# Attention products with 264 columns for 258, padded rows of the values and the probabilities, and 24 unread products at the end

## The reference, cut to what matters

```
h = layernorm(x) * (1 + ca) + sa
scores = einsum('nsd,ntd->nst', h * w_lhs, h * w_rhs)
attn = softmax(scores, axis=2)
x = x + ga * einsum('nst,ntd->nsd', attn, h)
h = layernorm(x) * (1 + cb) + sb
x = x + gb * (relu(h @ W1 + b1) @ W2 + b2)
```

## The kernel before, in words

| operand | starts at, modulo 256 |
|---|---|
| W1hi, W1lo, W2hi, W2lo (rows of G, weights of F) | 128 |
| hid_hi, hid_lo, h2hi, h2lo | 192 |
| Lhi, Llo, Rhi, Rlo | 64 |
| Phi[t], Plo[t], before | 64 |
| V[t] front half, V[t] rear half, before | 64 + 32 t, 80 + 32 t |
| Phi[t], Plo[t], changed | 128 + 64 t, 64 + 64 t |
| V[t] front half, V[t] rear half, changed | 64 + 64 t, 128 + 64 t |

## Time and profile before

### The profile page before, as it was taken

How to read it: one execution, slowest core, us unless ns; L and a number is a source line. 1 busy time by engine, 2 the same in 40 slices (tenths; PEclk the granted TensorE clock), 3 DMA queues, 4 the chain that set the end, 5 groups by cost and what they waited for, 6 DMA issues and landing times.

```text
span 672.1 us, 13438 instructions
## 1 busy us (share of the span) xinstructions
PE 665.8 (99%) x4481; PEld 612.9 (91%) x4481; DVE 549.5 (82%) x1139; ACT 513.4 (76%) x763; POOL 299.3 (45%) x311
## 2 busy tenths in 40 slices
PE   8999999999999999999999999999999999999998
PEld 8688898998999999999999989999899999999997
DVE  4799879998899789997899898998899977787321
ACT  2367779994899769995899948998599976677463
POOL 3471365155543364523547245352554333625444
PEclk9999999999999999999999999999999999999999
DMA  8141665237732578135662267513773246401300
GB/s 293 55 87 63 196 181 181 80 126 241 184 109 95 137 237 234 47 118 157 189 207 78 94 220 212 130 62 128 254 203 70 96 158 178 140 17 65 101 33 32
DMA packets 76929, 92.27 MB, mean 137 GB/s; under 512 B 9120, under 2 KB 67040, under 8 KB 76896
## 3 DMA queue, kind: packets, MB, share of 16 engines
q1 hardware_dynamic: 76896, 91.85, 45.4%
HBM read 55.33 MB, written 36.50 MB: 137 GB/s over the span
## 4 chain that ended last, share of the span: by engine, by line
PE 97%; DVE 2%; DMA 1%; issue 0%; SPq 0%; ACT 0%; DVEq 0%; ACTq 0%
PE col L675 9%; PE col L674 9%; PE col L673 9%; PE acc L595 8%; PE score L775 8%; PE acc L596 8%; PE acc L601 8%; PE score L771 8%; PE score L772 8%; PE score L663 4%; PE score L662 4%; PE score L664 4%; PE score L764 4%; PE score L636 2%; DMA S<-wmod 1%; PE score L751 1%
## 5 line engine op out<-in xcount | busy, mean ns | idle before, releaser
L1264 POOL TENSOR_TENSOR hid_lo<-hid,hid_hi 128x512 fp32r<-128x512 f32 x127 | 177.6, 1407 | 202.1 <-ACT hid_hi L800 201.7
L796 ACT ACTIVATE hid<-col,b1T 128x512 f32<-128x512 f32 x128 | 87.0, 679 | 69.9 <-PE col L675 65.2
L595 PE MATMUL acc<-W2hi,hid_hi 128*128 128x256 f32 x480 | 117.1, 278 | 0.0
L596 PE MATMUL acc<-W2lo,hid_hi 128*128 128x256 f32 x480 | 116.7, 278 | 0.0
L771 PE MATMUL score<-V,Phi 128*128 128x258 f32 x448 | 108.7, 281 | 0.0
L772 PE MATMUL score<-V,Phi 128*128 128x256 f32 x448 | 108.5, 281 | 0.0
L675 PE MATMUL col<-h2hi,W1lo 128*128 128x512 f32 x256 | 100.9, 394 | 0.0
L674 PE MATMUL col<-h2lo,W1hi 128*128 128x512 f32 x256 | 100.6, 393 | 0.0
L673 PE MATMUL col<-h2hi,W1hi 128*128 128x512 f32 x256 | 100.4, 392 | 0.0
L800 ACT ACTIVATE hid_hi<-hid 128x512 fp32r<-128x512 f32 x128 | 81.0, 633 | 15.3 <-PE acc L601 11.1
L595 PEld LDWEIGHTS acc<-W2hi,hid_hi 128*128 128x128 f32 x480 | 90.3, 188 | 2.5
(11 more groups left out here) (168 smaller groups left out, 1470.5 us busy)
## 6 DMA issues: line engine op xcount, KB each, us to landing
block_rows<-blocks SPq DMA_DIRECT2D x29, 512.0 KB, 2.6
blocks<-block_rows SPq DMA_DIRECT2D x116, 128.0 KB, 2.9
x_cur<-x SPq DMA_DIRECT2D x16, 512.0 KB, 4.1
ln_t<-x SPq DMA_DIRECT2D x14, 512.0 KB, 4.6
score_blocks<-stage SPq DMA_DIRECT2D x14, 512.0 KB, 3.0
S<-score_blocks SPq DMA_DIRECT2D x56, 128.0 KB, 3.6
S<-quarter_blocks SPq DMA_DIRECT2D x56, 96.0 KB, 2.3
out<-x_mlp SPq DMA_DIRECT2D x8, 512.0 KB, 3.6
```

The lines of the kernel that those rows point to most:

```text
L595: nc.tensor.matmul(o, hi, W2hi[:, it, :], start=(it == 0 and (apart or t % 2 == 0)), stop=False, skip_group_check=True)
L596: nc.tensor.matmul(o, hi, W2lo[:, it, :], start=False, stop=False, skip_group_check=True)
L796: nc.scalar.activation(hid[:, n % 2, :], col[n % 2][:], ACT.Relu, bias=b1T[:, n % FT:n % FT + 1]).then_inc(col_read, 1)
L1264: G.tensor_tensor(hid_lo[:, n % RING, :], hid[:, n % 2, :], hid_hi[:, n % RING, :].bitcast(F32), ALU.subtract).then_inc(hid_lo_done, 1)
```

## The change

- L771 and L775 stream 264 columns instead of 258, into PSUM tiles of 264 columns. Columns 258 to 263 of V are set to zero once, and their products are not read. The 8 of L772 keep 256 columns.
- Rows of V are 528 numbers (2112 bytes) instead of 520. The hi half, with the ones, now stands in front and the lo half 272 numbers (1088 bytes) behind it; L771 streams hi and L772 lo.
- Phi, Plo and `soft` are rows of 400 numbers (1600 bytes) for each t, which hold the three slots side by side. A tile of eight t is then eight pieces of 128, a row apart, for every instruction of ScalarE and VectorE on it.
- Small buffers move into the gaps and two are added, so that big buffers keep their distance to each other modulo 512 bytes, except the three rearranged ones (table above).
- `stage` and `stage_lr` now overlap every slot of Phi, so both waits stand before slot 0.
- Behind GT come 24 matmuls into `col[0]` that nobody reads: 8 of 258 columns, 8 of 260 and 8 of 256, of W2hi and W2lo with hid_hi and hid_lo as weights.

```diff
-    VW = D + 2
-    VP = D + 4
+    VW, VZ = D + 2, D + 8
+    VL, VROW = D + 16, 2 * D + 16
+    RROW = RING * P + 16
...
+        by_slot = lambda rows: rows[:, :, 0:RING * P].rearrange("p t (s c) -> p s t c", c=P)
...
-                nc.sbuf_tensor("stage_lr", [P, T, P], F32) as stage_lr, nc.sbuf_tensor("soft", [P, RING, T, P], F32) as soft:
-            stage_q = [q.rearrange("p a b -> p (a b)")[:, 0:Q * TURNS * QP] for q in (soft[:, RING - 1], stage_lr[:])]
-        Phi, Plo = sb("Phi", [P, RING, T, P], F32R), sb("Plo", [P, RING, T, P], F32R)
+        with nc.sbuf_tensor("stage", [P, 2, Q, HT, 2, QP], F32) as stage, nc.sbuf_tensor("stage_lr", [P, T, P], F32) as stage_lr, \
+                nc.sbuf_tensor("behind_stage", [P, 240], F32), nc.sbuf_tensor("soft_rows", [P, T, RROW], F32) as soft_rows:
+            soft = by_slot(soft_rows[:])
+            stage_q = [q[:].rearrange("p a b -> p (a b)")[:, 0:Q * TURNS * QP] for q in (soft_rows, stage_lr)]
+        Phi = by_slot(sb("Phi_rows", [P, T, RROW], F32R)[:])
+        mv2, nm2, rs2, nb2 = sb("mv2", [P, T, 2]), sb("nm2", [P, T]), sb("rs2", [P, T]), sb("nb2", [P, T])
+        sb("behind_Phi", [P, 72])
+        Plo = by_slot(sb("Plo_rows", [P, T, RROW], F32R)[:])
...
-        V = sb("V", [P, T, 2 * VP], F32R)
+        V = sb("V", [P, T, VROW], F32R)
...
-        av_ps = [score[0][:, 0:VW], score[0][:, HR:HR + VW]]
+        av_ps = [score[0][:, 0:VZ], score[0][:, HR:HR + VZ]]
...
+                        mv, unread = W2hi[:].rearrange("p i d -> p (i d)"), col[0]
+                        for width in (258,):
+                            for t in range(1, 5):
+                                cols = slice(t % HT * P, (t % HT + 1) * P)
+                                nc.tensor.matmul(unread[:, 0:width], hid_hi[:, 0, cols], mv[:, t * D - 2:t * D - 2 + width], start=True, stop=True)
+                                nc.tensor.matmul(unread[:, 0:D], hid_hi[:, 0, cols], W2lo[:, t, :], start=True, stop=True)
+                            for t in range(1, 5):
+                                cols = slice(t % HT * P, (t % HT + 1) * P)
+                                nc.tensor.matmul(unread[:, 0:width], hid_lo[:, 0, cols], mv[:, t * D - 2:t * D - 2 + width], start=True, stop=True)
...
                         for t in range(T):
-                            nc.tensor.matmul(o, Phi[:, slot, t, :], V[:, t, 0:VW], start=(t == 0), stop=False)
-                            nc.tensor.matmul(o[:, 0:D], Phi[:, slot, t, :], V[:, t, VP:VP + D], start=False, stop=False)
+                            nc.tensor.matmul(o, Phi[:, slot, t, :], V[:, t, 0:VZ], start=(t == 0), stop=False)
+                            nc.tensor.matmul(o[:, 0:D], Phi[:, slot, t, :], V[:, t, VL:VL + D], start=False, stop=False)
                         pe.wait_ge(plo_done, T * (b - 1) + n + 1)
                         for t in range(T):
-                            last = nc.tensor.matmul(o, Plo[:, slot, t, :], V[:, t, VP:VP + VW], start=False, stop=(t == T - 1))
+                            last = nc.tensor.matmul(o, Plo[:, slot, t, :], V[:, t, 0:VZ], start=False, stop=(t == T - 1))
...
-                        nc.scalar.activation(V[:, n * HT:(n + 1) * HT, VP:VP + D], ln_v[:], ACT.Copy).then_inc(v_hi, 1)
+                        nc.scalar.activation(V[:, n * HT:(n + 1) * HT, 0:D], ln_v[:], ACT.Copy).then_inc(v_hi, 1)
...
-                        if n == 1:
+                        if n == 0:
 
                             act.wait_ge(stage_stored[1], 16 * b)
-                        elif n == 2:
-
                             act.wait_ge(quarter_stored[1], 16 * b)
...
-                        for half in range(2):
-                            V_.memset(V[:, :, half * VP + D:half * VP + D + 1].bitcast(F32), 1.0)
-                            V_.memset(V[:, :, half * VP + D + 1:half * VP + VW].bitcast(F32), 0.0)
+                        V_.memset(V[:, :, D:D + 1].bitcast(F32), 1.0)
+                        V_.memset(V[:, :, D + 1:VZ].bitcast(F32), 0.0)
```

More of the change, by code:

```diff
@@ L279, in block_kernel @@
         lower = s_flat[:, at + 2 * TURNS * P:T * ROWS].rearrange("p (h u v t r) -> p h u v t r", h=2, u=Q, v=HT, t=2)
+        half_power, root_power = sb("half_power", [P, HT]), sb("root_power", [P, 2, DK])
         with nc.sbuf_tensor("W1_sb", [P, DK, FF], F32) as W1_sb, nc.sbuf_tensor("W2_sb", [P, FT, D], F32) as W2_sb:
             pass
[L286 to L289 removed]
+        by_slot = lambda rows: rows[:, :, 0:RING * P].rearrange("p t (s c) -> p s t c", c=P)
[7 more added lines that the diff above has]
+        Plo = by_slot(sb("Plo_rows", [P, T, RROW], F32R)[:])
         with nc.sbuf_tensor("L_first", [P, DK, ROWS], F32) as L_first, nc.sbuf_tensor("R_first", [P, DK, ROWS], F32) as R_first:
@@ L293, in block_kernel @@
         Rhi, Rlo = sb("Rhi", [P, DK, ROWS], F32R), sb("Rlo", [P, DK, ROWS], F32R)
-        with nc.sbuf_tensor("V_unsplit", [P, T, 2 * VP], F32) as V_unsplit:
-            V_first = V_unsplit[:, :, VP:VP + VW]
-        V = sb("V", [P, T, 2 * VP], F32R)
-        sb("behind_V", [P, 96])
+        with nc.sbuf_tensor("V_unsplit", [P, T, VROW], F32) as V_unsplit:
+            V_first = V_unsplit[:, :, 0:VW]
+        V = sb("V", [P, T, VROW], F32R)
+        nm1, rs1, nb1, row_max = sb("nm1", [P, T]), sb("rs1", [P, T]), sb("nb1", [P, T]), sb("row_max", [P, T])
         x_cur = sb("x_cur", [P, T, D])
@@ L692, in part @@
                             last.then_inc(tile_done, 1)
+                        mv, unread = W2hi[:].rearrange("p i d -> p (i d)"), col[0]
[7 more added lines that the diff above has]
+                                nc.tensor.matmul(unread[:, 0:width], hid_lo[:, 0, cols], mv[:, t * D - 2:t * D - 2 + width], start=True, stop=True)
+                        mv, unread = W2hi[:].rearrange("p i d -> p (i d)"), col[0]
+                        for width in (260,):
+                            for t in range(1, 5):
+                                cols = slice(t % HT * P, (t % HT + 1) * P)
+                                nc.tensor.matmul(unread[:, 0:width], hid_hi[:, 0, cols], mv[:, t * D - 0:t * D - 0 + width], start=True, stop=True)
+                                nc.tensor.matmul(unread[:, 0:D], hid_hi[:, 0, cols], W2lo[:, t, :], start=True, stop=True)
+                            for t in range(1, 5):
+                                cols = slice(t % HT * P, (t % HT + 1) * P)
+                                nc.tensor.matmul(unread[:, 0:width], hid_lo[:, 0, cols], mv[:, t * D - 0:t * D - 0 + width], start=True, stop=True)
                     elif kind == "MA":
@@ L750, in part @@
                         for t in range(HT):
-                            nc.tensor.matmul(av_ps[n], S[:, t, n * P:(n + 1) * P], V_first[:, t, :], start=(t == 0), stop=False)
+                            nc.tensor.matmul(av_ps[n][:, 0:VW], S[:, t, n * P:(n + 1) * P], V_first[:, t, :], start=(t == 0), stop=False)
                     elif kind == "AV":
@@ L763, in part @@
                                     pe.wait_ge(exp_done, n + 1)
-                                last = nc.tensor.matmul(o, S[:, t, n * P:(n + 1) * P], V_first[:, t, :], start=(t == 0), stop=(t == T - 1))
+                                last = nc.tensor.matmul(o[:, 0:VW], S[:, t, n * P:(n + 1) * P], V_first[:, t, :], start=(t == 0), stop=(t == T - 1))
                             last.then_inc(av_done, 1)
@@ L1147, in part @@
                         dve.wait_ge(v_hi, 2 * b + n - 1)
-                        V_.tensor_tensor(V[:, tiles, 0:D], ln_v[:], V[:, tiles, VP:VP + D].bitcast(F32), ALU.subtract).then_inc(v_done, 1)
+                        V_.tensor_tensor(V[:, tiles, VL:VL + D], ln_v[:], V[:, tiles, 0:D].bitcast(F32), ALU.subtract).then_inc(v_done, 1)
                     elif kind in ("BH", "B2"):
```

11 lines of the change are left out of this document (3 added, 8 removed).

## The result

The changed kernel takes 676.27 us (675.59 to 677.14, 10 runs) beside 674.67 us (673.88 to 675.86, 10 runs) of the kernel before on the same chip: ratio 1.0025 [1.0017, 1.0034]. It is slower by 0.25%, 1.6 us, where 4 us less were predicted. Its profiled execution took 676.63 us with a span of 674.8.

What follows compares the result with a forecast made beforehand. PE was taken to bound the kernel, busy 665.8 of 672.1 us. Terms -4.1 + 0.3 - 0.5 + 0.3 = -4.0 us gave a span of 668.1, plus 1.9 around it 670.0 us; range 668.9 to 675.0.

Steps and rivals of the forecast that it cites:

- Displacement: AV: next weights' start minus stream's start, modulo 256 bytes, becomes 64 for 22 of 24 matmuls; 256 columns then cost 113.3 ns.
- Width: L771 and L775: a column costs 0.45 ns, six added columns 0.043 us a tile, a 264-column product 116.9 ns.
- The tile: One AV tile of 24 matmuls: 2777 ns for 2850, on 56 tiles 4.1 us less.
- Neighbours: Around AV tiles: 0.3 us more at entry behind F, 0.5 us less at F behind AV, 0.3 us allowance.
- Does it reach the end?: Whole loop: PE's gain shortens the program, as Plo was ready 0.75 us before batch 3's first AV tile.
- New waits: ScalarE's first rounding of a batch waits for the stores of `stage` and `stage_lr`; no cost, 1.1 us in hand.
- Pieces of 128: VectorE and ScalarE operations on Phi, Plo and `soft`: cost zero, bounds plus and minus 0.02 us an operation.
- The end: Behind the last used product: 24 unread products take 2.7 to 2.9 us, hidden beside the stores by 0.4 us or more.
- the 0.5 us at F behind AV: 19 F stages following an AV tile each gain 0.03 us, 0.5 us less in all.
- the losses allowed for: 0.3 us more where tiles follow F, and 0.3 us for batch 1's waiting and products keeping part of their excess.
- the margin of 0.75 us: Batch 3's first AV tile: its Plo was ready at 266.51 and used at 267.26.
- Rival 1: L771 and L775: displacement does nothing, added columns cost 0.043 us a tile, 2.4 us, giving 676.4; chance 0.08.

Runs made afterwards that it cites:

- the bench: Changed kernel with 19 chains behind settling products replacing its unread ones; at its own addresses a tile took 2820 ns with 256 columns, 2887 with 264.
- both narrow ones: Only each AV tile's first product has 258 columns, the others 256: on the changed kernel 674.56 us, on the kernel before 673.03 us.
- the first chains: Kernel before with 24 chains of unread products behind its last used one, varying width, displacement and streamed row; 256 columns at displacement 64 could come at 113.3 ns.

## Why the prediction was wrong

**Displacement**, the first step, failed: "If G's pitch follows from that, a product of 256 columns costs 113.3 ns." It does not follow. 113.3 is one of two pitches at which 256 columns at displacement 64 repeat, and which of them holds is decided by what came before, down to one product of 258 columns. The trace before held a warning that the prediction read and used only in one rival: F, at one displacement throughout, came at 233.3 and at 228.3. G's 34 stretches of at least 24 all at 113.3 were one history seen many times, not 34 confirmations. What a tile at the new addresses costs with 256 columns is 2820 in the bench and 2813 to 2835 in the kernel with narrow products (its first product is wider), where the step has 24 x 113.3 = 2719: by the bench 101 ns of the 111 by which the tile missed.

**Width** was sized nearly right from the wrong base. It had 16 x 3.6 = 58 ns for 8 columns on a product; at these addresses the bench shows 2887 - 2820 = 67. For the six that the change added it had 0.043 us a tile, and measured were 33 ns. But the price depends on place: in the old rows the same six cost up to 2922 - 2852 = 70 ns a tile.

**The tile** was then 2888 instead of 2777, and 35 above before instead of 73 below: +1.96 us instead of -4.1.

**Neighbours**, **Does it reach the end?**, **New waits**, **Pieces of 128** and **The end** held within 0.3 us, in part by luck: the 0.5 us at F behind AV came to 0.1 at most with 264 columns, but the losses allowed for did not come either. With 258 columns all of them together made 0.9998 [0.9988, 1.0007], without the unread products nothing changed. One limit: the margin of 0.75 us before the first AV tile is gone in some executions, of the changed kernel and of both narrow ones among others.

Rival 1 comes nearest, 676.4 for 676.27: the displacement does nothing and the columns cost. It had 8 in 100. It had the price and the place; its own reason, 24 products into one bank, is not what the runs show, since 32 into one bank came at 113.3 in the first chains. The rule N/2.4 + 2.5 ns from the Trainium skill, page "TensorE: Matmul & The Clock Gate", section "Back-to-back issue gap", would have given 2.2 us more, an estimate from that page; 1.85 were measured for the columns. The rule has no term for addresses, and the section gives it for a product by itself and other spacings for a stream of weight loads and products, which the prediction did not say. It had the sign and nearly the size, though not the pitches: 258 columns would be 110 ns by it, and 119 to 121 were measured, and for it 113.3 and 117.9 at the same addresses can't both be.

What stays open is the mechanism. The runs show that a pitch can take more than one value at one set of addresses, and what moved it from one to the other; not which part of the chip holds that state, nor a rule from residues to the pitch of a mixed tile. No simple function of the displacement fits the tables above.

## What to carry to other kernels

A pitch that repeats all over a trace may be a state that its neighbours set: before an address rule is built on it, find in the trace, or make in a bench behind the real predecessors, the same products after another history and at the width that is meant. Extra columns for the sake of alignment are paid for at once, the alignment may give nothing. And when a layout is moved, compare the pitches of the stages that were not touched: here G, whose operands had not moved, lost 1.3 of the 1.9 us that the moved tiles had gained.

## What the runs showed of the hardware

All at the full granted clock (2.4 GHz), split products of 128 rows and 128 weights:

- 256 columns repeat at 113.3 ns or at 117.7 to 117.9, same operands and addresses, and stay there for 24 products and more. One product of 258 columns ahead of 24 moved them from the shorter to the longer; behind one of 288, and in a chain with weights from another tensor, they came back from the longer to the shorter. In one kernel the longer pitch held for over 40 us, through F as well as G.
- 256, 258 and 260 to 272 columns cost 113.3, 121.2 and 123 to 124.4 at displacement 64 with a changing row: the first two columns above 256 cost up to 8 ns (3 if 256 stand at the longer pitch), the next fourteen 2 to 3.
- 512 columns, whose displacement 64 is the slowest shown (233.7, with 227.3 at 0), rank the residues the other way round than 256 do.
- A tile of 24 mixed products at one set of residues takes 2830, 2848 or 2856 ns by the stage ahead of it, the same in every batch.
